# Three receiver tiles of the last group gathered by SyncE, row by row, in a graph network layer with residual and normalization

## The reference, cut to what matters

```python
edge_feat = concat([h[receiver], h[sender], rel_pos, distance])       # 25000 x 260
x1 = silu(edge_feat @ W1 + b1); x2 = silu(x1 @ W2 + b2)
scores = (x2 @ W3 + b3)[:, 0]
alpha = softmax of scores over the edges of one receiver
msg = h[sender] @ Wv * (alpha * node_weight[sender])[:, None]
out = layernorm(h + segment_sum(msg, receiver))                        # 100000 x 128
```

## Time and profile before

| | |
|---|---|
| median of 3 runs | 998.13 us (997.67 to 998.24) |
| the profiled execution, first to last instruction (span) | 996.1 us |
| the median less that span | 2.0 us |
| GpSimd busy | 752.3 us (76%), 790 instructions |
| TensorE busy | 575.9 us (58%) |
| VectorE busy | 573.2 us (58%) |
| ScalarE busy | 522.6 us (52%) |
| mean granted TensorE clock | 0.820 of full |

### The profile page before, as it was taken

One profiled execution on the slowest core, in us unless ns is written; L12 is line 12 of the kernel. 1 busy time (PEld: TensorE's weight loads), 2 busy tenths in 40 slices (PEclk: granted clock), 3 DMA queues, 4 the chain that ended last, 5 costly groups with the idle time before them and its releaser, 6 DMA issues.

```text
span 996.1 us, 10941 instructions
## 1 busy us (share of the span) xinstructions
PE 575.9 (58%) x2587; PEld 394.8 (40%) x2587; DVE 573.2 (58%) x2275; ACT 522.6 (52%) x1168; POOL 752.3 (76%) x790
## 2 busy tenths in 40 slices
PE   0989999988704457677667666777996600000000
PEld 0656766665502223455445444545675500000000
DVE  6987887773452737597698987953678841000000
ACT  0356655554523756777698979974786630000000
POOL 6777777777777777777777777777777777777777
PEclk9999999999998776788788988878999855555555
DMA  7799999989965877788778878763452231111111
GB/s 208 227 302 315 321 320 333 336 233 311 330 226 161 288 256 245 273 292 268 273 272 283 292 234 317 246 185 91 129 124 79 71 78 53 53 51 52 53 53 45
DMA packets 85079, 206.12 MB, mean 207 GB/s; under 512 B 19797, under 2 KB 56566, under 8 KB 72472
## 3 DMA queue, kind: packets, MB, share of 16 engines
q1 hardware_dynamic: 56728, 140.95, 41.7%
q0 software_dynamic: 28288, 64.48, 22.8%
HBM read 113.16 MB, written 92.31 MB: 206 GB/s over the span
## 4 chain that ended last, share of the span: by engine, by line
POOL 38%; issue 23%; PE 20%; ACT 13%; DVE 5%; DMA 0%; POOLq 0%; ACTq 0%; DVEq 0%
POOL hk L422 23%; POOL out_rows L426 15%; ACT xin L478 6%; PE bank L622 5%; PE bank L638 4%; PE bank L645 3%; PE bank L624 2%; ACT hk L530 2%; PE bank L616 2%; PE bank L609 2%; ACT hkT L501 1%; ACT x L511 1%; ACT zs L521 1%; PE bank L597 1%; DVE dst L899 1%
## 5 line engine op out<-in xcount | busy, mean ns | idle before, releaser
L478 ACT ACTIVATE xin<-xin,drs 128x128 f32<-128x128 f32 x637 | 258.1, 484 | 51.6 <-DVE drs L884 51.5
L422 POOL DMA_INDIRECT hk<-in_xw,snd_t x196 | 188.0, 959 | 62.0 <-issue 59.4
L426 POOL DMA_INDIRECT out_rows<-hk,sidx_t x196 | 188.8, 963 | 59.7 <-issue 59.4
L422 POOL DMA_INDIRECT region<-rec_d,id_t x196 | 186.8, 953 | 59.7 <-issue 59.1
L422 POOL DMA_INDIRECT hk<-in_x,kg_t x196 | 186.6, 952 | 59.7 <-issue 59.7
L899 DVE BATCH_NORM_STATS2 dst<-xin 128x6 f32<-128x256 f32 x392 | 137.0, 414 | 61.6 <-DMA xin<-in_x 61.0
L577 PE MATMUL bank<-w1b,region 128*128 128x128 f32 x392 | 149.1, 484 | 13.8 <-ACT region L488 7.8
L622 PE MATMUL bank<-hkT,w1a 128*128 128x512 f32 x98 | 73.2, 839 | 138.8 <-issue 98.3
L577 PEld LDWEIGHTS bank<-w1b,region 128*128 128x128 f32 x392 | 99.8, 315 | 33.9 <-ACT region L488 10.1
L622 PEld LDWEIGHTS bank<-hkT,w1a 128*128 128x128 f32 x98 | 20.1, 240 | 175.5 <-issue 163.2
L511 ACT ACTIVATE x<-bank,bcol 128x512 f32<-128x512 f32 x49 | 33.5, 683 | 95.0 <-PE bank L624 95.0
(11 more groups left out here) (176 smaller groups left out, 853.0 us busy)
## 6 DMA issues: line engine op xcount, KB each, us to landing
xin<-in_x SPq DMA_DIRECT2D x49, 1024.0 KB, 8.2
out_rows<-xin SPq DMA_DIRECT2D x49, 1024.0 KB, 5.2
rec_d<-hk SPq DMA_DIRECT2D x49, 514.0 KB, 7.7
krow<-seg_d SPq DMA_DIRECT2D x49, 128.0 KB, 3.5
hk<-in_xw,snd_t POOLq DMA_INDIRECT x196, 5.8
hk<-in_x,kg_t POOLq DMA_INDIRECT x196, 3.9
region<-rec_d,id_t POOLq DMA_INDIRECT x196, 3.6
out_rows<-hk,sidx_t POOLq DMA_INDIRECT x196, 2.2
```

Of the source, the lines that this page charges most:

```text
L422: pool.indirect_dma_start(out=to, out_offset=None, in_=frm, in_offset=bass.IndirectOffsetOnAxis(ap=index, axis=0)).then_inc(done, 16)
L426: pool.indirect_dma_start(out=out, out_offset=bass.IndirectOffsetOnAxis(ap=index, axis=0), in_=frm, in_offset=None).then_inc(done, 16)
L478: ins = nc.scalar.activation(xin[:, j % X_RING, n, :], xin[:, j % X_RING, n, :], ACT.Identity, bias=drs[:, j % 2, 1, n:n + 1], scale=drs[: ...
```

## The change

Three tiles of the last group, T-4, T-3 and T-2 (192, 193 and 194 of 0 to 195), are left out of GpSimd's hk gathers. SyncE stores their columns of `kg_t` to a small DRAM tensor, at the end of the first phase. In the second phase, after `dense(B0 + s)`, it issues 12 DMAs of one row of x each, with the row's number from a register, in each of the first 32 steps (3 x 128 = 384 rows). Every 24 rows it first loads the next 24 numbers into its registers. Before the first of them it waits until all records have left the ring that lies over this part of `hk`, and until the table is in DRAM. TensorE waits for these rows through a semaphore of their own before it turns group 48.

```diff
+KEPT_TILES = (T - 4, T - 3, T - 2)
+KEPT_READ, KEPT_ROWS = 24, 12
...
+            sp.wait_ge(S["tab_ready"], 1)
+            sp.dma_start(kept_d.rearrange("o (t p) -> p (o t)", p=P), kg_t[:, KEPT_TILES[0]:KEPT_TILES[-1] + 1],
+                         allow_slow_non_contiguous=True).then_inc(S["kept_out"], 16)
+
+            def receiver_rows():
+                for r in range(HS_RING):
+                    sp.wait_ge(rec_out[r], 16 * len(range(r, G, HS_RING)))
+                sp.wait_ge(S["kept_out"], 16)
+                for o in range(0, len(KEPT_TILES) * P, KEPT_READ):
+                    _, rows = nc.values_load_multi_w_load_instructions(
+                        kept_d[0:1, o:o + KEPT_READ], [mybir.EngineType.SP], min_val=0, max_val=N - 1,
+                        skip_runtime_bounds_check_because="receivers are rows of x, those of the padding too")
+                    for n, r in enumerate(rows, o):
+                        t, p = KEPT_TILES[n // P], n % P
+                        sp.dma_start(hk[p:p + 1, t // TPG, t % TPG, :], x[bass.ds(r, 1), :]).then_inc(S["hk_rows"], 16)
+                        yield
...
                 dense(B0 + s)
+                for _ in range(KEPT_ROWS):
+                    next(receivers, None)
...
-                        gather(hk[:, g, q, :], x, kg_t[:, t:t + 1], hk_in[g % HK_SEMS])
+                        if t not in KEPT_TILES:
+                            gather(hk[:, g, q, :], x, kg_t[:, t:t + 1], hk_in[g % HK_SEMS])
...
             def turn_rows(g):
-                wait_ring(pe, hk_in, g, 16 * TPG)
+                if g == G - 1:
+                    pe.wait_ge(hk_in[g % HK_SEMS], 16 * (TPG * (g // HK_SEMS + 1) - len(KEPT_TILES)))
+                    pe.wait_ge(S["hk_rows"], 16 * P * len(KEPT_TILES))
+                else:
+                    wait_ring(pe, hk_in, g, 16 * TPG)
```

More of the change, by code:

```diff
@@ L129, in gnn_kernel @@
     yl_d = nc.dram_tensor("yl_d", (T, H), F32).ap()
+    kept_d = nc.dram_tensor("kept_d", (1, len(KEPT_TILES) * P), I32).ap()
     with ExitStack() as ctx:
@@ L245, in gnn_kernel @@
             "parts_ready", "parts_out", "fix_ready", "fixT_done", "fexp_ready", "fexp_done", "fixY_ready", "fixY_done",
-            "fix_stats", "chain_f", "fix_res", "fix_out")}
+            "fix_stats", "chain_f", "fix_res", "fix_out", "kept_out", "hk_rows")}
         hs_in = [sem(f"hs_in{r}") for r in range(HS_RING)]
@@ L385, in store_y @@
                                  ).then_inc(y_out[g % Y_SEMS], 16)
+            receivers = receiver_rows()
             for s in range(LAST_STEP):
```

## The result

The changed kernel takes 1024.99 us (median of 4 runs, 1023.92 to 1027.27) beside 997.90 us for the kernel before on the same chip: 1.0273 of it, 95% interval 1.0259 to 1.0288. It is slower by 27 us, not faster by 2. The profiled execution has a span of 1023.5 us, 27.4 more than before.

What follows compares the result with a forecast made beforehand. GpSimd's count of indirect DMAs by 1.26 us, plus stalls, was taken as the bound. Span 996.1 less 2.1 for the removed gathers, SyncE's added work hidden, gave 994.0; plus 2.0 for the runs' median, 996.0 us; range 994.3 to 1012.

Steps and rivals of the forecast that it cites:

- part 2: SyncE's queue: the added rows and register loads cost 5.9 us a step, bounds 3.5 and 10.5, right at the edge.
- The price of a register load: SyncE's load of 24 numbers, in every second step: 3.0 us taken, between 0.24 and 5.8.
- The price of a row: SyncE's one-row DMA with a register address, 12 a step: 0.37 us taken, between 0.28 and 0.63.
- A: The forecast itself for the whole kernel: 996.0 us (995.6 to 996.6), chance 45%.
- case D: SyncE becomes the bound; late blocks hold up VectorE, TensorE and the gathers: 1012 us at 6.8 a step, chance 31%.
- The free time of SyncE: SyncE's waits from 310 to 640 us that rows can fill: 185.9 us over 33 steps, 5.6 a step.
- The slacks of 8.6 and 13.6 us: Room to absorb SyncE's lateness: 8.6 us before a dense block is read, 13.6 us in GpSimd's ring of 12.
- Part 1: GpSimd's tail: three removed gathers free 3.75 us, but TensorE stops the last gathers; 2.1 us pass to the end.
- B: The full gain: TensorE runs step 39 at the upper clock and GpSimd isn't stopped, 994.4 us, chance 10%.
- What the text said would prove it wrong: VectorE waiting for in_x between 400 and 640 us, or gathers waiting for TensorE's L645 before 700 us.
- One sign of being right: SyncE's waits for ScalarE's norm falling from 155 to under 50 us.
- the single DMA engine for one-partition transfers: 12 rows of 512 B on the lowest-numbered DMA engine add an estimated 0.8 us to each block load, inside slack.

Runs made afterwards that it cites:

- e12: The change with 10 rows a step over 39 steps in place of 12 over 32, loads of 24 every 2.4 steps: 1.0027 of the kernel before.
- e11: The change with 12 numbers to a register load and a load in every step, same rows in all: 1.0368 of the kernel before.
- e10: The change with the 384 row numbers read from one partition of SBUF in place of DRAM: 1.0011 of the kernel before, 998.05 us.
- e1: The change with the three tiles gathered by nobody (left out of the computation), SyncE only storing the table: 0.9949 of the kernel before.
- e9: The change with its rows and loads put between the store of one dense block and the load of the next: 0.9965 of the kernel before.
- e2: The change with its 384 row DMAs at fixed addresses, without register loads or register arithmetic (tiles hold other rows): 0.9968 of the kernel before.
- e4: The change with its 16 loads kept but one row DMA behind each, the other 368 rows left out: 0.9958 of the kernel before.
- e5: The change with the three tiles gathered by nobody, plus a scatter group behind each of r39 to r48: 0.9960 of the kernel before.
- e8: The change with 6 rows a step to step 31, 16 in steps 35 to 46, and scatters between r39 to r48: 0.9961 of before, 994.76 us.
- e6: The kernel before with only its scatters dealt between r39 to r48, all receiver tiles on GpSimd: 1.0005 of the kernel before.
- e3: The change with the 24 registers loaded once at step 0 and used 16 times (tiles hold other rows): 0.9964 of the kernel before.

## Why the prediction was wrong

**The step that failed** is in part 2, the issue time added to SyncE's queue: 5.9 us a step forecast, 7.7 measured. Two terms of the sum fell short, by 0.9 us a step each. The price of a register load ("nothing is nearer to one than to the other, so 3.0") measured 4.8 us (mean of 16; median 5.0): 2.4 a step, not 1.5. The price of a row ("I take 0.37, a quarter of the way") measured 0.41 where nothing held it up, since an address costs two more instructions, and 0.44 with the row DMAs that were held up: 5.3 a step, not 4.4. The prediction had itself found that the edge lay at 5.6. The middle of an unknown price had been put beside an edge to a tenth of a us, and A was called likeliest for want of a row.

The Trainium skill's figure ("Runtime: NRT & Kernel Launch", Instruction fetch mechanics: about 200 ns a register) gives an estimated 4.8 us for 24, and the change's trace shows that as its mean. The prediction named it as the sentence that spoke against, gave 6.8 us a step by it, put case D there, and left D at 31%. Other runs here don't bear out a fixed price a register: the same 24 numbers from DRAM took 4.0 us by the mean in e12, 12 of them 2.9 in e11, and 24 from SBUF mostly 1.63 in e10.

**The free time of SyncE was right**: 5.6 a step, and the experiments bracket it (4.7 costs nothing, 6.2 does). The slacks of 8.6 and 13.6 us weren't tested singly. **Rival D** was right in every link: rows and loads, late blocks and key rows, L928 and L996 on VectorE, z, the gathers. With the measured 7.7 its own sum is (7.7 - 5.6) by 32 = 67 us late. The trace shows 56; part of the difference is that SyncE's waits for its own stores shrank too, from 77.3 to 60.2 us, for which the sum had no term. 56 less the 22.2 of both slacks is 34 us, and GpSimd's stalls are 32.9. Its 1012 was low through the same two prices.

**Part 1** (the removal is worth 2.1 us) has its mechanism shown by e1's profile, with r48 at 736.74 (e9's has the like, 3.3 us in five waits), and its size not: the stalls there were larger than forecast, and e1's runs gained 3.7 to 6.4 us. It wasn't a fixed number either: where TensorE comes to step 39 at the upper clock (e2 to e4), or with the scatters dealt in between (e5, e8), GpSimd has no stall. B at 10% was too low, and "nothing changes that" was wrong: TensorE's idle time before step 39 was 4.82 us in the profile of before and 1.60 in e6, where all that stands ahead of it is the same.

**What the text said would prove it wrong** came true: VectorE waits for in_x between 400 and 640 us, and gathers wait for L674 before 700 us. One sign of being right came true as well, SyncE's waits for ScalarE's norm under 50 us (10.6), but it came from a queue that was full.

One of the two citations had no weight: the single DMA engine for one-partition transfers (the Trainium skill, "DMA: Bandwidth & Descriptors", Why a DMA increments its semaphore by 16 and not by 1). The example given there is a single value and not a row of 512 bytes, but the profiles fit one engine for a row as well, with 768 packets more on SyncE's queue in the change than in e1 (57,896 and 57,128), two for each of the 384 rows. Which engine took them no row of a trace shows; e2 and e3 show that 384 of them cost nothing there.

## What to carry to other kernels

An engine that shows much idle time may still have little room: take its waits of a stretch, leave out those for its own transfers, divide by the steps, and hold the added issue time against that, instruction by instruction and with something on top: here 12 rows that need 4.9 us took 5.3 on average. If a price without a row decides between two cases and the sum lies on the edge, neither middle nor hope is a price: give the higher bound the larger chance, or move the work so that the price doesn't matter, as between a store and the load that waits for it. And before taking work from the bound engine, look which engine takes over right behind: here TensorE's 5.55 us steps in the tail, which didn't stop GpSimd any more once the scatters were dealt in between.

## What the runs showed of the hardware

- A SyncE register load of 24 numbers from DRAM took 4.8 us on average in the change (2.8 to 6.1) and 4.0 in e12 (2.9 to 5.7), one of 12 numbers 2.9 us (e11), one of 24 from a partition of SBUF mostly 1.63 us (e10). What stands behind it on SyncE's queue starts after it: load and first row at 603.76 + 5.83 and 609.76.
- A one-row DMA whose source comes from a register costs SyncE 0.41 us from start to start (0.037 + 0.029 + 0.228 and gaps), one with a fixed address 0.29 us (3.53 / 12). Some of the 384 took over 0.4 us to issue, up to 1.33 us: 1 in e11, 13 in the change, 31 in e2; e2's came to 0.36 us a row on average, the change's to 0.44.
- A GpSimd gather that waits for z starts 0.3 to 0.6 us after it: in e1 group 36's z ended at 736.13 by the modelled end of its matmuls, r48 started at 736.74; group 35's ended at 730.58, r47 started at 730.85.
- TensorE took 2.05 us for L648 after 3.97 us of idle time and 1.10 us for the same product (L651) after 0.86 us, at the same place of two kernels that do the same work there. In the kernel before and e9 it was 2.05 after 4.82 and 4.75 us of idle time, in e2, e4, e5 and e6 1.10 after 1.19 to 1.60.
